# One unrolled program over four streams, with attention and feed-forward halves in alternation, in place of a loop over pairs of streams

## What is computed

```python
x = x + tanh(g_xattn[0]) * L0_xattn(_layernorm(x), ctx)     # 16 heads of 8, mask over (token, key)
x = x + tanh(g_ffn[0])   * L0_ffn(_layernorm(x))            # 64 small two-layer nets, inner width 16
x = x + tanh(g_xattn[1]) * L1_xattn(_layernorm(x), ctx)     # 16 heads; a temperature per head from
...                                                         # mean, max and variance of the scores
x = x + tanh(g_ffn[1])   * L1_ffn(_layernorm(x))            # 4 experts, 128 to 512, silu gate, top 2
x = x + tanh(g_xattn[2]) * L2_xattn(_layernorm(x), ctx)     # 16 heads, mask over keys
x = x + tanh(g_ffn[2])   * L2_ffn(_layernorm(x))            # second norm, 8 experts, 128 to 352, top 2
x = x + tanh(g_xattn[3]) * L3_xattn(_layernorm(x), ctx)     # one head of 128, relu projections
x = x + tanh(g_ffn[3])   * L3_ffn(_layernorm(x))            # 8 linear experts, top 2
```

## Time and profile before

| | us |
|---|---|
| runs | 1236.43, 1242.81, 1242.48; median 1242.48 |
| span of the profiled execution | 1233.0 (9.5 below the median) |
| PE busy, weight loads | 1048.9 (85%), 569.6 (46%) |
| DVE, ACT, POOL busy | 653.2 (53%), 514.2 (42%), 110.2 (9%) |
| mean granted clock of PE | 0.836 |
| prologue, until the first body | 90.3 |
| first body to last F3 body, pass 1 and pass 2 | 528.7 and 530.4 |

### The profile page before, as it was taken

How to read it: one execution, slowest core, us unless ns; L and a number is a source line. 1 busy time by engine, 2 the same in 40 slices (tenths; PEclk the granted TensorE clock), 3 DMA queues, 4 the chain that set the end, 5 groups by cost and what they waited for, 6 DMA issues and landing times. The chain is left out here.

```text
span 1233.0 us, 12606 instructions
## 1 busy us (share of the span) xinstructions
PE 1048.9 (85%) x3833; PEld 569.6 (46%) x3833; DVE 653.2 (53%) x1914; ACT 514.2 (42%) x1177; POOL 110.2 (9%) x176
## 2 busy tenths in 40 slices
PE   1469978789999899996877997779998989999697
PEld 1344433346554455664324443345555445566432
DVE  0765275746664466553426428664665436665332
ACT  0525567763325634332003557864433463433200
POOL 3100021300000110000000003220000011000000
PEclk8679996589997799996567999759999679999655
DMA  9100000000000000000000000000000000000000
GB/s 277 33 21 1 1 1 1 1 1 1 1 0 1 1 1 1 1 1 0 1 17 22 1 1 0 1 1 1 1 1 0 1 1 1 1 1 1 0 1 17
DMA packets 11653, 12.66 MB, mean 10 GB/s; under 512 B 3337, under 2 KB 7486, under 8 KB 11582
## 3 DMA queue, kind: packets, MB, share of 16 engines
q10 hardware_dynamic: 5536, 8.04, 2.2%
q1 hardware_dynamic: 5662, 3.24, 1.0%
q0 software_dynamic: 384, 0.53, 0.2%
HBM read 10.75 MB, written 1.05 MB: 10 GB/s over the span
## 5 line engine op out<-in xcount | busy, mean ns | idle before, releaser
L850 ACT ACTIVATE PT<-bank 128x512 f32<-128x512 f32 (+1 forms) x160 | 95.5, 597 | 261.4 <-PE bank L1436 261.3
L1156 DVE TENSOR_TENSOR PT<-PT 128x512 f32<-128x512 f32 (+1 forms) x160 | 110.3, 690 | 177.7 <-ACT PT L850 177.6
L1434 PE MATMUL bank<-Qs,m_w_lo 128*128 128x512 f32 (+1 forms) x320 | 173.9, 543 | 0.0
L1450 PE MATMUL bank<-PT,m_w 128*128 128x512 f32 (+1 forms) x320 | 168.1, 607 | 4.1 <-DVE PT L1160 3.5
L1436 PE MATMUL bank<-Qs,m_w_hi 128*128 128x512 f32 (+1 forms) x320 | 127.4, 398 | 0.0
L1435 PE MATMUL bank<-Qs,m_w_hi 128*128 128x512 f32 (+1 forms) x320 | 127.1, 397 | 0.0
L1373 PE MATMUL bank<-Qs,KT 112*77 112x512 f32 x192 | 106.1, 600 | 12.0 <-ACT PT L812 7.5
L1258 PE MATMUL bank<-KT,Qs 96*128 96x308 f32 x192 | 86.4, 476 | 31.0 <-ACT Eb L759 27.9
L1160 DVE TENSOR_TENSOR PT<-PT,bank 128x512 f32<-128x512 f32 (+1 forms) x160 | 109.8, 686 | 5.5
L1029 DVE TENSOR_REDUCE nm<-bank 128x4 f32<-128x308 f32 x192 | 85.1, 471 | 24.5 <-PE bank L1266 13.0
L671 POOL TENSOR_SCALAR rstd<-mv 128x4 f32<-128x4 f32 x32 | 9.3, 292 | 934.9 <-DVE mv L902 934.9
(11 more groups left out here) (264 smaller groups left out, 1628.1 us busy)
## 6 DMA issues: line engine op xcount, KB each, us to landing
nat_m<-in_L_ffn_W_dram ACTq DMA_DIRECT2D x1, 1408.0 KB, 15.3
m_w<-in_L_ffn_w_dram ACTq DMA_DIRECT2D x1, 1024.0 KB, 11.1
raw_w<-in_L_ffn_w_dram ACTq DMA_DIRECT2D x1, 1024.0 KB, 12.4
x<-in_x_dram SPq DMA_DIRECT2D x4, 256.0 KB, 3.7
out_dram<-x SPq DMA_DIRECT2D x4, 256.0 KB, 2.0
f_out<-in_L_ffn_Wout_dram POOLq DMA_DIRECT2D x8, 64.0 KB, 7.6
m_w<-in_L_ffn_W_experts_dram ACTq DMA_DIRECT2D x1, 512.0 KB, 16.7
ctxn<-in_ctx_dram SPq DMA_DIRECT2D x4, 38.5 KB
```

The source lines that it names most:

```text
L850: act.activation(hb[n % 3][0:m, :], bank[(2, 3, 6)[2 * n % 3]][0:m, :], ACT.Silu).then_inc(*chunk_act.up(u, n))
L1156: op = dve.tensor_tensor(h, h, shares[e % 2][0:m, :], ALU.mult)
L1434: pe.matmul(dst, w_lo, x_hi, start=True, stop=False)
L1450: pe.matmul(bank[5][:], wd, hb[n % 3][0:m, :], start=n == 0, stop=n == len(todo) - 1) \
```

## The change

`STREAMS` becomes 4 and the loop goes: all 32 units stand in one program, and the loads of the four streams are issued together at its start, their stores at the end. `order()` writes the sequence: A A, then F and A in turn, with each stream's F one unit behind its A by `LAG = 2`. Written with the stream behind the point: A0.0 A0.1 F0.0 A0.2 F0.1 A0.3 F0.2 A1.0 F0.3 A1.1 F1.0 A1.2 F1.1 A1.3 F1.2 A2.0 F1.3 A2.1 and so on, until A3.3 F3.2 F3.3. Buffers of a unit are no longer doubled by stream but by `side`: 0 for A, 1 for F (the last F has side 0). x, the context and the masks have one buffer for each stream; KT, VP, nm and others that only A units use have one in all. Where a unit and the next have the same side (A0.0 and A0.1), the next is prepared behind the first, not beside it (`apart`). Waits that named the unit before by `u - 1` or `u - STREAMS` now find it with `earlier`. The steps of `pre`, `body` and `tail`, `later` and the rule for `start` stay as they are. The final barrier goes too.

In the diff, repeated edits of the kind `x[s]` to `x[b]` are left out.

```diff
--- before.py
+++ after.py
@@ -39,7 +39,8 @@
 B = 4
-STREAMS = 2
+STREAMS = 4
+SIDES = 2
@@ -54,6 +55,8 @@
 UNITS = 2 * LAYERS * STREAMS
+HALVES = LAYERS * STREAMS
+LAG = 2
@@ -67,8 +70,36 @@
+def order():
+    done = [("A", i) for i in range(LAG)]
+    for i in range(HALVES):
+        done.append(("F", i))
+        if i + LAG < HALVES:
+            done.append(("A", i + LAG))
+    return done
+ORDER = order()
 def kind(u):
-    return "AF"[(u // STREAMS) % 2] + str(u // STREAMS // 2)
+    half, i = ORDER[u]
+    return half + str(i // STREAMS)
+def stream(u):
+    return ORDER[u][1] % STREAMS
+def side(u):
+    return int(kind(u)[0] == "F" and u + 1 < UNITS)
+def earlier(u, kinds, of=None):
+    return next((w for w in range(u - 1, -1, -1) if kind(w) in kinds and of in (None, stream(w))), None)
@@ -164,9 +195,9 @@
-        KT = [sb(f"KT{s}", [QK + H, H, S2], F32R) for s in range(STREAMS)]
-        VP = [sb(f"VP{s}", [S2, H, 32]) for s in range(STREAMS)]
-        lg = [sb(f"lg{s}", [P, T, LG]) for s in range(STREAMS)]
+        KT = sb("KT", [QK + H, H, S2], F32R)
+        VP = sb("VP", [S2, H, 32])
+        lg = [sb(f"lg{s}", [P, T, LG]) for s in range(SIDES)]
@@ -355,18 +386,16 @@
                                    pattern=[[32, 4], [HD, J]], channel_multiplier=-1).then_inc(*const.up("quad"))
-                for s in range(STREAMS):
+                for b in range(STREAMS):
+                    pool.memset(ctxn[b][:, P:P + 1], 1.0)
+                for s in range(SIDES):
                     pool.memset(lg[s][:], PAD)
-                    pool.memset(ctxn[s][:, P:P + 1], 1.0)
-                    pool.memset(VP[s][:], 0.0).then_inc(*zeroed.up("values", s))
-                    pool.wait_ge(*zeroed.at("values", s))
-                    pool.memset(VP[s][:, :, HD:HD + 1], 1.0)
+                pool.memset(VP[:], 0.0)
                 pool.wait_ge(*zeroed.at("last"))
-                for s in range(STREAMS):
-                    pool.tensor_copy(KT[s][QK:QK + H, :, :], ident[QK:QK + H, QK:QK + H].unsqueeze(2).to_broadcast([H, H, S2])) \
-                        .then_inc(*zeroed.up("heads", s))
-                    pool.wait_ge(*zeroed.at("heads", s))
+                pool.tensor_copy(KT[QK:QK + H, :, :], ident[QK:QK + H, QK:QK + H].unsqueeze(2).to_broadcast([H, H, S2])) \
+                    .then_inc(*zeroed.up("heads"))
+                pool.wait_ge(*zeroed.at("heads"))
@@ -491,11 +520,14 @@
     def two(name, shape, dt=F32):
-        return [sb(f"{name}{s}", shape, dt) for s in range(STREAMS)]
-    x = two("x", [P, T, P])
+        return [sb(f"{name}{s}", shape, dt) for s in range(SIDES)]
+    def each(name, shape, dt=F32):
+        return [sb(f"{name}{b}", shape, dt) for b in range(STREAMS)]
+    x = each("x", [P, T, P])
     ctxn = v["ctxn"]
-    ctxT = two("ctxT", [P, S2])
+    ctxT = each("ctxT", [P, S2])
...
@@ -580,16 +612,12 @@
         "oT_ready result_psum stored").split())
-    mine = sorted(s.num for s in (in_x[0].sem, stored.sem))
-    to_clear = range(mine[0], mine[1] + 1)
-    xv = a["x"].rearrange("(i s) (p t) d -> i s p t d", s=STREAMS, t=T)
-    ov = out.rearrange("(i s) (p t) d -> i s p t d", s=STREAMS, t=T)
-    cv = a["ctx_1024"].rearrange("(i s) k d -> i s k d", s=STREAMS)
-    ik = a["mask_BxS2_ik0"].rearrange("(i s) k -> i s k", s=STREAMS)
-    jf = a["mask_BxS2_if1"].rearrange("(i s) k -> i s k", s=STREAMS)
+    xv = a["x"].rearrange("s (p t) d -> s p t d", t=T)
+    ov = out.rearrange("s (p t) d -> s p t d", t=T)
+    cv, ik, jf = a["ctx_1024"], a["mask_BxS2_ik0"], a["mask_BxS2_if1"]
     MHA = ("A0", "A1", "A2")
+    KINDS = tuple(half + str(l) for half in "AF" for l in range(LAYERS))
@@ -634,7 +662,8 @@
             t, ends = (steps_tail(kind(u - 1)), tail(u - 1)) if later(u - 1) else (0, iter(()))
-            m, first = (0, iter(())) if last else (steps_pre(kind(u + 1)), pre(u + 1))
+            apart = not last and side(u + 1) == side(u)
+            m, first = (0, iter(())) if last or apart else (steps_pre(kind(u + 1)), pre(u + 1))
@@ -644,28 +673,30 @@
             assert sent == m and all(next(part, None) is None for part in (ends, main_part, first))
-    it = ctx.enter_context(nc.Fori(0, B // STREAMS))
+            if apart:
+                for _ in pre(u + 1):
+                    pass
     with nc.Block() as block:
             for s in range(STREAMS):
-                sp.dma_start(x[s][:], xv[it, s]).then_inc(*in_x[s].up("all", by=16))
-                sp.dma_start(ctxn[s][:, 0:P], cv[it, s]).then_inc(*in_ctx[s].up("all", by=16))
+                sp.dma_start(x[s][:], xv[s]).then_inc(*in_x[s].up("all", by=16))
+                sp.dma_start(ctxn[s][:, 0:P], cv[s]).then_inc(*in_ctx[s].up("all", by=16))
                 for i, m in enumerate((ik, jf)):
-                    sp.dma_start(mk_i[s][:, i:i + 1], m[it, s].rearrange("(k o) -> k o", o=1)).then_inc(*in_mask[s].up(i, 0, by=16))
-                    sp.dma_start(mr_i[s][:, i, :], m[it, s].rearrange("(o k) -> o k", o=1)).then_inc(*in_mask[s].up(i, 1, by=16))
+                    sp.dma_start(mk_i[s][:, i:i + 1], m[s].rearrange("(k o) -> k o", o=1)).then_inc(*in_mask[s].up(i, 0, by=16))
+                    sp.dma_start(mr_i[s][:, i, :], m[s].rearrange("(o k) -> o k", o=1)).then_inc(*in_mask[s].up(i, 1, by=16))
             for s in range(STREAMS):
-                sp.wait_ge(*x_done.at(UNITS - STREAMS + s))
-                sp.dma_start(ov[it, s], x[s][:]).then_inc(*stored.up(s, by=16))
+                sp.wait_ge(*x_done.at(earlier(UNITS, ("F3",), s)))
+                sp.dma_start(ov[s], x[s][:]).then_inc(*stored.up(s, by=16))
             sp.wait_ge(*stored.at(STREAMS - 1))
             def pre(u):
-                s, k = u % STREAMS, kind(u)
+                s, k, b = side(u), kind(u), stream(u)
...
@@ -724,21 +755,21 @@
                         if i == 1 and k == "A0":
-                            if u >= 1 and kind(u - 1) == k:
-                                act.wait_ge(*keys_ready.at(u - 1, J - 1))
+                            if earlier(u, MHA) is not None:
+                                act.wait_ge(*keys_ready.at(earlier(u, MHA), J - 1))
                                                bias=bcol[0:QK, l, 1, g:g + 1],
-                                               accum_out=ksum[s][0:QK, g:g + 1] if l == 1 else None).then_inc(*k_high.up(u, g))
+                                               accum_out=ksum[0:QK, g:g + 1] if l == 1 else None).then_inc(*k_high.up(u, g))
                             act.wait_ge(*v_psum.at(u))
...
@@ -847,6 +878,8 @@
                             act.wait_ge(*ffn_psum.at(u, n - 3))
+                        elif n == 0 and kind(u - 1) == "A3":
+                            act.wait_ge(*out_psum.at(u - 1, 0))
@@ -877,8 +910,8 @@
                 dve.wait_ge(*out_turned.at(u, g))
-                if g == 0 and u >= 1 and kind(u - 1) in MHA:
-                    dve.wait_ge(*att_turned.at(u - 1))
+                if g == 0 and earlier(u, MHA) is not None:
+                    dve.wait_ge(*att_turned.at(earlier(u, MHA)))
...
@@ -1001,16 +1035,16 @@
                                                          op0=ALU.add, op1=ALU.subtract).then_inc(*k_low.up(u, g))
-                        if i == 5 and l != 1:
+                        if i == 5:
                             dve.wait_ge(*v_psum.at(u))
-                            dve.wait_ge(*masks_ready.at("all", s))
-                            dve.tensor_copy(VP[s][:, :, HD:HD + 1],
-                                            (mk[s][:, 1:2] if l == 2 else ones[0:S2, 0:1]).unsqueeze(2).to_broadcast([S2, H, 1]))
+                            dve.wait_ge(*masks_ready.at("all", b))
+                            dve.tensor_copy(VP[:, :, HD:HD + 1],
+                                            (mk[b][:, 1:2] if l == 2 else ones[0:S2, 0:1]).unsqueeze(2).to_broadcast([S2, H, 1]))
                             dve.wait_ge(*k_low.at(u, G - 1))
...
@@ -1082,17 +1116,17 @@
                             dve.wait_ge(*temp_scalar.at(u, 2))
-                            if u >= 1 and kind(u - 1) == k:
-                                dve.wait_ge(*probs_ready.at(u - 1, H - 1))
+                            if earlier(u, ("A1",)) is not None:
+                                dve.wait_ge(*probs_ready.at(earlier(u, ("A1",)), H - 1))
...
@@ -1532,8 +1566,6 @@
-    nc.all_engine_barrier(sems_to_clear=to_clear)
```

167 lines of the change are left out of this document (84 added, 83 removed).

## The result

The changed kernel takes 1265.2 us (median of four runs, 1258.2 to 1274.9) against 1242.6 for the kernel before (1236.4 to 1244.7): a ratio of 1.0195, 95% interval 1.0141 to 1.0249, 22.6 us slower. The forecast was 1260.

A forecast was written before the change was run, and what follows sets the result against it. Limits differ by stretch: PE's work in F1 and F2, DVE's pace in A1 preparation, half clock from A3 on. Layers +41.6, +18.6, -22.2, -18.6, less 1.7, give +17.7: span 1250.7, time 1260 us, range 1249 to 1270.

The forecast's parts named there:

- two large costs: Layers 0 and 1: late preparation start in F0 bodies, and F1 bodies with A1 preparation; layers forecast +41.6 and +18.6 us.
- F0|A1: F0 body with A1 preparation beside it: preparation starts only at the seventh step, 54.2 us each, twice 108.4.
- The first A0: Layer 0, first unit: body 14.5, tail 6.1 and a preparation with nothing beside it, 17.5 at full clock; 38.1 us.
- F1|A1: F1 body with A1 preparation: 34.5 us, five ACT/DVE cycles of 7.6, then 10; 83 us each, ends 56.4 and 95.9.
- F1|A2: F1 body with A2 preparation: 57.2 us plus 2 for an attention tail replacing a feed-forward one, 59.2 each.
- 2 for the tail: F1 body with A2 preparation: attention tail replacing a feed-forward one, between 0 and 6.1 us, PE doing mostly small transposes.
- A2|F: A2 body with feed-forward preparation: 17.3 us instead of 18.8, since it follows a dense feed-forward body; four times, 69.2.
- F3|A3: F3 body with A3 preparation: 28.7 + 1.9 for PE work + 1.4 for its own tail, 32.0 us, twice 64.0.
- The first (F1|A1 under 70): Engines overlap there as totals allow: DVE's 56.4 us a unit, 1207 us in all; chance 0.20 with all other shrinking stretches.
- the second (71 to 77): F1 bodies with A1 preparation overlap partly: 71 to 77 us a unit, 1236 to 1248 us in all; chance 0.13.
- The third, half clock in the new stretches: PE falls to half clock in the new stretches; five cycles 4.5 us more, 1275 us in all; chance 0.09.
- The table switch at twice its price: Ten ACT table switches in each of two units at twice 1.28 us add 26 us, 1286 us; chance 0.03.

The follow-up runs named there:

- e1: Changed kernel, but in the four F0 bodies the next attention unit's preparation starts at the first step instead of the seventh: 1241.6 us.
- e3: Changed kernel with ReLU in place of SiLU in the F1 and F2 chunks: 1242.5 us.
- e7: Changed kernel with the 24 DVE reductions of exponentials and squares in each A1 preparation replaced by four-column copies: 1259.6 us.
- e8: Changed kernel with both the DVE reductions replaced by four-column copies and ReLU in place of SiLU: 1221.1 us.
- e12: Kernel of e1 with all sixteen blocks of an A1 preparation treated as the odd ones, DVE subtracting maxima and summing exponentials: 1249.5 us.
- e4: Kernel before without its loop: four streams unrolled in the old order, first pair's buffers reused by the second: 1223.0 us.
- e2: Changed kernel, but in every F body with a delayed attention tail the preparation starts with the first step: 1246.9 us.
- e10: Kernel of e1 with five unused matmuls behind the third scores of each A1 and A2 body that follows an F body: 1259.5 us.
- e11: Kernel of e1 with the preparation beside F1|A1 sent in every second chunk only: 1244.3 us.
- e5: Kernel of e1 with ACT tables loaded early by one-element activations before F1, F2, A2 and A3 bodies: 1246.7 us.
- e9: Kernel of e4 with 64 unused matmuls behind A3's scores and in three steps of F3's preparation: 1240.0 us.

## Why the prediction came out as it did

**Sign and size.** 1260 against 1265.2, slower, within the range. The two large costs stood where they were put, and the balance of the rest was partly luck: two errors of 25 and 20 us, in layers 2 and 3, cancelled.

**F0, right.** Forecast F0|A0 31.5 and F0|A1 54.2; measured 32.5 and 51.2. The cause, the start at the seventh step, is shown by e1. The price of F0|A1 was 3 high.

**The first A0.** 38.1 forecast, 41.9 measured: I took the apart preparation at full clock, and the stretch had 0.84.

**F1|A1, right in the main.** 83 forecast, 81.2 and 80.1 measured. The forecast's cycle of 7.6 us came out at 6.6 to 7.4, 14.0 for two chunks; by its own terms it is 6.9 or 7.7, by the kind of the last block. Of its two table loads the forecast had one on the path and the other beside DVE's two blocks, so 6.4 us in five cycles; e3, without twelve loads, is 6.2 and 5.1 us shorter, which agrees (the 64 to 70 us expected of e3 counted most of the fourteen). The path itself is not quite the one written out: in every second cycle it holds no load and goes through PE, from the block's score matmul to the next chunk's. That DVE and ACT stand in turn on it is what the chain shows; e7, e8 and e12 fit, but their cuts were small. A1|F stretches were 19.1 on average against 20.2.

**F1|A2, mis-sized.** 59.2 forecast, 64.2 and 66.7 measured. The term that failed is "2 for the tail". In e4 the same body without an attention tail takes 57.2 at clock 1.00; here PE is busy 59.0 and 61.6 with 0.97 and 0.91. At clock 1.00 (e1) the term is 5.9: the forecast's reason, "PE does mostly small transposes there", put the work too low (2.8 us) and left out the idle time (3.1 us), of which some 1.7 us go with the late start (e2), priced for F0 and not here. The same tail stands in F2|A2 (81.0 against 78.8) and F2|A3 (68.3 and 67.4 against 65.2, with no term for it), 9.7 us together.

**A2|F, mis-sized, four times.** 17.3 forecast, 20.7 to 21.4 measured: 16 us. The step "now it follows a dense feed-forward body, so I take 17.3" was wrong. The body begins with a wait for the first exponentials, and the clock falls behind it; e10 shows that at 0.99 it would still be 19.8. Without table loads (e3) it is 19.3 to 19.7, at clocks of 0.77 to 0.83. So clock and load are worth about 1 us each, and the rest of the miss is the body itself: no run here has it under 18.8. The row of before, 18.8, had another attention body ahead of it, no table load, and a wait of 0.5 us; its clock was at 0.50 from the body ahead.

**F3, mis-sized the other way.** F3|A3 forecast 32.0, measured 26.3 and 23.4, at clock 0.65 and 0.74: 14 of the 20 us. I had priced it from F3|F3 at 0.52. The row I took the price from was at half clock almost throughout; with an A3 preparation in it and another body ahead, it wasn't.

**The offset.** "the median of the runs is 9.5 us above that, which I carry over" mixed two things: 1.8 us lie outside a span, and the rest is that this execution was fast. The medians moved by 22.6 where I had said 17.7, the profiled spans by 31.9.

**The rivals.** The first (F1|A1 under 70) is refuted, and the second (71 to 77) with it; even without loads it is 75. The third, half clock in the new stretches, didn't happen in F1|A1 (0.86 and 0.89), but the clock was low in others: 0.75 in F0|A1, 0.84 in the first A0, 0.72 in an A0|F0 that took 3.9 us more for it. The table switch at twice its price is refuted by e3: twelve loads fewer gave 0.5 us each.

**Open.** What the shortest order for F1|A1 is; e2, e11 and e12 each changed one knob and none shortened it. What part of e1's 24 us is the clock was not separated. Why e5 is 5 us slower than e1 wasn't followed to its end. An alternation only in layer 3, where it gained 10 to 19 us, wasn't tried.

## To carry to other kernels

When a preparation is moved into another body, look first at where in that body it may begin: the rule that cost 16 us or more in a body of eleven steps cost nothing in F1|A1, with nineteen, where starting at once (e2) took 9 us more. Look also at the tail that comes with the new neighbour: in F1|A2 an attention tail in place of a feed-forward one, with the later start that it brings, took 6 us, where 2 were allowed. Pair a stage that is bound by TensorE with one that uses the others; F1 and A1 both lean on DVE and ACT in turn, and interleaved they took longer than each with its own kind. And take the parts of a change singly: here unrolling was worth 1.5%, and the reordering that came with it cost more than twice that.

## What the runs showed of the chip

TensorE can be busy all the time and stay at half clock. In e4's F3.0|F3.1, PE busy without a gap for 20 us:

```profile
590.00:595.00 5.00, 5.00 (x6) 1.55 (x6) 3.27 (x14) 0.00 (x0) 1.27 (x2) 0.50 0.00 0
595.00:600.00 5.00, 5.00 (x9) 2.17 (x9) 1.38 (x2) 0.60 (x1) 0.00 (x0) 0.50 0.00 0
600.00:610.00 10.00, 10.00 (x20) 4.57 (x19) 3.30 (x19) 0.23 (x1) 0.00 (x0) 0.50 0.00 1
```

In the whole stretch the granted clock was 0.53; in e9, with matmuls added in it and in the waits ahead of it, it was 0.94, and e9 entered it at 1.00 where e4 entered it at 0.50. Which of the additions did it wasn't told apart.

The same code also took 14.6 or 18.4 us (A0|F0) and 22.1 or 25.9 us (F3.2|F3.3) from one kernel to the next, at clocks of 1.00 or 0.72, and 0.72 or 0.57. The four runs of the changed kernel, spans 1256.5, 1262.0, 1264.9 and 1273.2 us, had mean clocks of 0.848, 0.844, 0.841 and 0.835. A difference of a few us in one stretch says nothing before its clock is read.
